# One core, four fused layers: how the attention sums of two query tiles are turned and divided

## The reference, cut to what matters

```
scores = einsum('bhid,bhjd->bhij', q, k) / 4 + alibi        # 16 heads, 2048 x 2048
scores = where(causal, scores, -inf)
attn   = softmax(scores, axis=-1)
out    = einsum('bhij,bhjd->bhid', attn, v)                 # 16 numbers a head
x      = layernorm(x + out.reshape(b, l, 256) @ o_w)
```

## Time and profile before

| | us |
|---|---|
| median of three runs | 1425.99 (1423.18 to 1426.55) |
| the profiled execution | 1421.0 |
| its span in the profile | 1419.2 |
| PE busy | 1369.9 |
| DVE busy | 1064.5 |
| ACT busy | 870.5 |

### The profile page before, as it was taken

One profiled execution on the slowest core, in us unless ns is written; L12 is line 12 of the kernel. 1 busy time (PEld: TensorE's weight loads), 2 busy tenths in 40 slices (PEclk: granted clock), 3 DMA queues, 4 the chain that ended last, 5 costly groups with the idle time before them and its releaser, 6 DMA issues. The chain is left out here.

```text
span 1419.2 us, 44173 instructions
## 1 busy us (share of the span) xinstructions
PE 1369.9 (97%) x18460; PEld 844.3 (59%) x18460; DVE 1064.5 (75%) x2004; ACT 870.5 (61%) x1775; POOL 264.2 (19%) x436
## 2 busy tenths in 40 slices
PE   7999999999999999999999999899997799999998
PEld 4554334444444444444444445687876689999997
DVE  2567888988888888888888881356687676777775
ACT  3445658778787787787787877655465333333332
POOL 4332111102111111121011100000256611111111
PEclk9999999999999999999999999999998799999999
DMA  7695411112212212121300000312705555454441
GB/s 224 206 214 122 84 19 37 46 32 49 47 33 48 46 33 47 34 47 41 83 23 3 3 3 2 117 31 91 258 29 191 209 186 183 179 185 178 164 181 70
DMA packets 77824, 134.08 MB, mean 94 GB/s; under 512 B 12226, under 2 KB 64443, under 8 KB 72252
## 3 DMA queue, kind: packets, MB, share of 16 engines
q1 hardware_dynamic: 59612, 108.84, 25.9%
q10 hardware_dynamic: 14608, 14.00, 3.1%
q0 software_dynamic: 3408, 8.43, 1.7%
HBM read 67.75 MB, written 23.11 MB: 64 GB/s over the span
## 5 line engine op out<-in xcount | busy, mean ns | idle before, releaser
L1611 ACT ACTIVATE big<-pair 128x512 f32<-128x512 f32 (+1 forms) x1120 | 584.9, 600 | 184.3 <-PE pair L1244 175.1
L1799 DVE TENSOR_REDUCE part_max<-pair 128x2 f32<-128x1024 f32 (+2 forms) x576 | 643.2, 1161 | 72.6 <-PE pair L1216 43.6
L1244 PE MATMUL pair<-big 128*32 128x512 bf16 (+3 forms) x5120 | 344.9, 349 | 3.4 <-DMA big<-max_t 2.6
L1216 PE MATMUL pair<-big 128*32 128x512 bf16 (+3 forms) x5120 | 341.0, 349 | 4.5 <-DVE part_max L1799 4.0
L1266 PE MATMUL pair<-big 128*17 128x512 f32 (+3 forms) x2560 | 288.0, 528 | 0.7 <-POOL big L2228 0.3
L1216 PEld LDWEIGHTS pair<-big 128*32 128x32 bf16 x5120 | 124.9, 96 | 185.3 <-DVE part_max L1799 87.7
L1244 PEld LDWEIGHTS pair<-big 128*32 128x32 bf16 x5120 | 123.2, 96 | 157.0 <-ACT big L1611 71.6
L1624 ACT ACTIVATE std<-moments,eps_col 128x1 f32<-128x1 f32 (+1 forms) x110 | 32.5, 295 | 218.4 <-DVE moments L1837 218.3
L1502 PE MATMUL pair<-big,tok 128*128 128x128 f32 x1248 | 147.6, 277 | 4.8 <-DVE big L2112 4.8
L1502 PEld LDWEIGHTS pair<-big,tok 128*128 128x128 f32 x1248 | 146.9, 194 | 7.6 <-DVE big L2112 5.7
L2228 POOL TENSOR_SCALAR_AFFINE_SELECT big<-big 128x512 f32<-128x512 f32 x128 | 80.1, 635 | 331.1 <-ACT big L1611 331.1
(11 more groups left out here) (184 smaller groups left out, 1280.1 us busy)
## 6 DMA issues: line engine op xcount, KB each, us to landing
tok<-big SPq DMA_DIRECT2D x39, 1024.0 KB, 4.7
big<-in_L_ffn_w SPq DMA_DIRECT2D x16, 1024.0 KB, 13.7
big<-split_dram SPq DMA_DIRECT2D x216, 64.0 KB, 2.8
split_dram<-big ACTq DMA_DIRECT2D x32, 384.0 KB, 4.0
big<-split_dram SPq DMA_DIRECT2D x42, 256.0 KB, 4.2
big<-routed_dram SPq DMA_DIRECT2D x39, 129.0 KB, 2.1
tok<-in_L_attn_x SPq DMA_DIRECT2D x8, 512.0 KB, 6.0
big<-in_c_query_rows SPq DMA_DIRECT2D x8, 512.0 KB, 4.8
```

What stands on the lines that cost most here:

```text
L1216: mm = pe.matmul(bank[q:q + STRIPE, o:o + w], m.q_op[slot][:, step.qt, h, step.r * P + q:step.r * P + q + STRIPE], m.k_op[slot][:, h, step ...
L1244: mm = pe.matmul(m.bank[step.bank][k:k + STRIPE, n * w:(n + 1) * w], m.k_op[slot][:, h, step.kb * P + k:step.kb * P + k + STRIPE], m.q_op[ ...
L1611: act.activation(m.p_ring[:, step.place, step.heads[0]:step.heads[-1] + 1, step.at:step.at + w], m.bank[step.bank][:, 0:len(step.heads) * ...
L1799: dve.tensor_reduce(m.part_max[(step.u * QT + step.qt) % 2][:, step.r, step.heads[0]:step.heads[0] + n, step.c], banks[:, :, 0:w], X, ALU. ...
```

## The change

Divide is done once for two query tiles, t even and t + 1, when the sums of the second have been taken. PE then makes eight transposes, four from each `acc_t`, into the two banks of one slot; DVE inverts and multiplies over both banks in one instruction each. The order is planned anew with 1070 ns of PE and 950 ns of DVE for it. POOL waits at the start of the back until the ring has been taken, since `acc_t[0]` is now read by the last Divide.

```
 # FrontPlan.take_sums
-        self.to_divide.append((t, self.sums_at))
+        if t % 2:
+            self.to_divide.append((t - 1, self.sums_at))
 # FrontPlan.divide
-        self.divided_ring[t] = n
-        self.steps.append(Divide(t // QT, t % QT, t, n, room))
-        self.pe += 640
-        self.dve = max(self.dve, self.pe + self.PE_LAG) + 600
+        self.divided_ring[t] = self.divided_ring[t + 1] = n
+        self.steps.append(Divide(t // QT, t % QT, t, t // 2, n, room))
+        self.pe += 1070
+        self.dve = max(self.dve, self.pe + self.PE_LAG) + 950
 # tensor_front
-            a = step.t % 2
-            pe.wait_ge(s.sums_taken, step.t + 1)
+            pe.wait_ge(s.sums_taken, step.t + 2)
             wait_room(pe, s, step.room)
-            for r in range(BPT):
-                mm = pe.transpose(m.bank[MAX_BANKS[step.room.slot][0]][:, r * P:(r + 1) * P], m.acc_t[a][:, r * P:(r + 1) * P],
-                                  m.ident[:, :])
+            for a, b in enumerate(MAX_BANKS[step.room.slot]):
+                for r in range(BPT):
+                    mm = pe.transpose(m.bank[b][:, r * P:(r + 1) * P], m.acc_t[a][:, r * P:(r + 1) * P], m.ident[:, :])
             mm.then_inc(s.ring_filled, 1)
 # vector_front
-            view = m.bank[MAX_BANKS[step.room.slot][0]].rearrange("p (r h n) -> p r h n", r=BPT, h=GH)
+            view = m.max_tile[step.room.slot][:, :].rearrange("p (r h n) -> p r h n", r=2 * BPT, h=GH)
...
-            dve.wait_ge(s.inverted, step.t + 1)
+            dve.wait_ge(s.inverted, step.n + 1)
             dve.tensor_tensor(dst, view[:, :, :, 0:HD], m.recip_l[:, :, :].unsqueeze(3)
-                              .broadcast_to([P, BPT, GH, HD]), ALU.mult).then_inc(s.ring_taken, 1)
+                              .broadcast_to([P, 2 * BPT, GH, HD]), ALU.mult).then_inc(s.ring_taken, 1)
 # pool_back
     pool.wait_ge(s.sums_taken, len(UNITS) * QT)
+    pool.wait_ge(s.ring_taken, plan.front_ring)
     pool.memset(m.ones_b, 1.0).then_inc(s.onesb_set, 1)
```

More of the change, by code:

```diff
@@ L95 @@
 TakeSums = namedtuple("TakeSums", "t weighed divided_before")
-Divide = namedtuple("Divide", "u qt t ring room")
+Divide = namedtuple("Divide", "u qt t n ring room")
 Residuals = namedtuple("Residuals", "ring")
@@ L364, in take_sums @@
         self.sums = None
+        assert t < 2 or t - 2 in self.divided_ring
         self.steps.append(TakeSums(t, weighed, self.divided_ring.get(t - 2, -1) + 1))
@@ L929, in __init__ @@
         self.max_t = [sb(f"max_t{i}", [3 * MAXIMA, P], BF16) for i in range(2)]
-        self.recip_l = sb("recip_l", [P, BPT, GH])
+        self.recip_l = sb("recip_l", [P, 2 * BPT, GH])
         self.stats = sb("stats", [P, NORMS, BPT, 6])
@@ L1040, in __init__ @@
                        for i in range(W1_AHEAD)]
-        self.gate = self.recip_l[:, :, :].rearrange("p a b -> p (a b)")
+        self.gate = self.recip_l[:, 0:BPT, :].rearrange("p a b -> p (a b)")
     def group(self, g):
@@ L1819, in vector_front @@
             b, g = UNITS[step.u]
-            view = m.bank[MAX_BANKS[step.room.slot][0]].rearrange("p (r h n) -> p r h n", r=BPT, h=GH)
+            view = m.max_tile[step.room.slot][:, :].rearrange("p (r h n) -> p r h n", r=2 * BPT, h=GH)
             blk = b * BPB + step.qt * BPT
-            dst = m.tok[:, blk:blk + BPT, g * GH * HD:(g + 1) * GH * HD].rearrange("p r (h n) -> p r h n", h=GH)
+            dst = m.tok[:, blk:blk + 2 * BPT, g * GH * HD:(g + 1) * GH * HD].rearrange("p r (h n) -> p r h n", h=GH)
             dve.wait_ge(s.ring_filled, step.ring + 1)
             dve.reciprocal(m.recip_l[:, :, :], view[:, :, :, HD]).then_inc(s.inverted, 1)
-            dve.wait_ge(s.inverted, step.t + 1)
+            dve.wait_ge(s.inverted, step.n + 1)
             dve.tensor_tensor(dst, view[:, :, :, 0:HD], m.recip_l[:, :, :].unsqueeze(3)
-                              .broadcast_to([P, BPT, GH, HD]), ALU.mult).then_inc(s.ring_taken, 1)
+                              .broadcast_to([P, 2 * BPT, GH, HD]), ALU.mult).then_inc(s.ring_taken, 1)
 def take_moments(dve, m, s, i, rows):
```

## The result

| | before | after |
|---|---|---|
| median, 7 runs each | 1423.18 us | 1415.45 us |
| ratio, with its 95% interval | | 0.9942 [0.9927, 0.9957] |
| profiled execution | 1421.0 | 1415.08 |
| its span | 1419.2 | 1413.3 |

That the gain is twice as large does not come from the base. The size is wrong, and what the size came from is wrong too. In two kernels of the experiments (e10, e12) one execution took 2153 and 2068 us; these two are left out of the ratios.

What follows compares the result with a forecast made beforehand. PE was taken to bound the attention, with ACT beside it from 872 us. PE -3.7, DVE -0.4 and tail net +0.36 summed to -3.7 us: from 1425.99 to 1422.3, range 1416 to 1430.

Steps and rivals of the forecast that it cites:

- the repeating units: Attention's four-tile units of 95.5 us: PE busy 95.2 to 95.45, so only 0.05 to 0.4 us idle to win.
- A pair gives back 0.28 us: PE time saved per merged Divide, taken as 0.26; 14 pairs give 3.64 us, -3.7 with the first pair.
- The plan stays about as true as it was: Planned prices fall 210 ns of PE and 250 of DVE a pair, near the trace's 260 and 430.
- the 11 us of slack a unit: DVE, busy 84.2 of 95.5 us mid-run, hides both its 0.43 us saving and 0.43 us longer wait per pair.
- The multiply at 0.692 us: DVE's multiply over both banks (128x512), priced from a tensor_tensor of that size; bounds 0.425 and 0.85.
- The reciprocal at 0.275: DVE's reciprocal of 32 instead of 16 numbers, at 1.04 ns an element; bounds 0.258 and 0.516 us.
- The tail, +0.72: The last Divide, fully on the path, grows by 0.43 of transposes, 0.02 of reciprocal and 0.27 of multiply.
- The early stretch, -0.4: Between 147 and 190 us PE waits for the ring, so DVE's saving counts there; bounds 0 and -0.7.
- The clock, 2 us either way: The whole back moves some 4 us against the granted clock, so a low stretch may lie elsewhere.
- the order filling holes: Rival, chance 0.20: new order also takes half of PE's 7.6 us idle between 118 and 334 us; 1418.5 us.
- Given back at the ring: Rival, chance 0.18: PE waits for the slot as long as it saved; only the tail left, 1426.4 us.
- The slower rival: Chance 0.12, with other bad orders: maxima come too late, PE waits 1.32 us in 8 more tiles; 1432.9 us.

Runs made afterwards that it cites:

- e10: Changed kernel, its order planned with the merged Divide at 950 ns of PE and 720 of VectorE instead of 1070 and 950; ratio 0.9929 to the kernel before.
- e12: Kernel before, single Divides, its order planned with 750 ns of VectorE instead of 600, PE left at 640; ratio 0.9948 to the kernel before.
- e1: Kernel before's list of steps with even Divides taken out, pairs merged where the odd ones stood, slots handed out anew; ratio 1.0047 to the kernel before.
- e5: Kernel before, single Divides, its order planned with 700 ns of PE and 750 of VectorE instead of 640 and 600; ratio 0.9942 to the kernel before.
- e3: Changed kernel, with VectorE inverting and multiplying each of the two banks by itself; ratio 0.9962 to the kernel before.
- e9: Kernel before, single Divides, its order planned with 800 ns of PE and 900 of VectorE instead of 640 and 600; ratio 1.0027 to the kernel before.
- e14: Kernel before, single Divides, its order planned with 820 ns of VectorE instead of 600, PE left at 640; ratio 1.0016 to the kernel before.

## Why the prediction was wrong, step by step

PE's share in the piece was priced right; the step that failed is the reading that the repeating units had nothing to win.

- "A pair gives back 0.28 us ... I take 0.26": right. The Divides' surcharge fell by 2.6 us over 10 pairs in the old order (e1), by 2.2 in the new.
- "In the repeating units there is next to nothing to win (0.05 to 0.4 us of idle PE a unit)": this step failed. There were 6.7 us of short waits in five units, 1.3 a unit, and 4.7 of them are gone in the changed kernel's order; e12, which changes the order alone, has 1.6 us left and the whole gain. I had written that a busy PE says nothing, looked at a few groups, and then took the busy time for the bound on idleness after all. Added up over the unit, the distances from start to start would have given the 1.3.
- That merging by itself pays, with the order as a risk beside it: failed as well. In the old order the five units are 2.0 us longer with merging (e1), though each Divide costs less. An order alone, with single Divides, gives as much as the change (e5, e12).
- "The plan stays about as true as it was": so it did. VectorE's price fell short of the measured time by 0.24 us for two single Divides, and by 0.14 for a pair. The order changed nearly everywhere all the same.
- "In the middle of the run the 11 us of slack a unit hide both" (VectorE's two times): half right. Splitting VectorE's work again cost 1.7 us in five units (e3), so it is not all hidden.
- The multiply at 0.692 us: right, 0.692. The reciprocal at 0.275: wrong, it is 0.357, since 16 more numbers took 0.099 us, 6.2 ns each, not the multiply's 1.04. I had put the slope of another operation to it; the bounds held it. The pair takes 1.09 on VectorE, saving 0.35 and not 0.43, so 5.6 us over the run. Without the gaps the two instructions add up to 5.0 us less over the run, and VectorE's busy time on the page of the profile, where instructions that overlap count once, fell by 3.6, where I had said 6 to 7.
- The tail, +0.72: 0.80, by that same reciprocal. Net with the last unit I said +0.36; the last unit, which was to win 0.36, lost 0.4.
- The early stretch, -0.4: -0.5 to TakeSums 3. That this has the right size is luck: the granted clock differed there (0.83 against 1.00 between 184 and 194 us), a difference in clock goes with 1.5 us in e5's two profiles, and the new order has its part in it too. No run separates them.
- The clock, 2 us either way: +1.4 net, of -2.7 and +4.1.
- The base: the median before was 1423.18 and not 1425.99 us. My forecast difference from there gives 1419.5, still 4 us too slow.
- The rivals: the one that came nearest was the order filling holes, but I looked for the holes in the early stretch, and capped them there at half of 7.6 us. "Given back at the ring" came in e1's five units, for one half at the ring and for the other at ACT. The slower rival did not come by late maxima; e9 and e14 are slower by more and longer short waits.

The rule of the Trainium skill that I weighed ("Perfetto Trace Analysis", section "Optimizing Scalar/DVE Operations": breaking instructions up may help where Vector isn't saturated and causes bubbles on others) is not borne out here: e3 breaks them up and is 2.4 us longer in the front. It is a weak test, since e3's pieces all wait for the eight transposes and free the slot after the last one, so that nothing is done sooner. Another rule of that page (section "Identifying the Most-Contended Engine") says that the matmuls' busy share is no good measure of how close a kernel is to its roofline. The trace agrees as far as it goes: 95.45 of 95.5 us busy, and 1.5 us a unit were to be had.

## What to carry to other kernels

Where matmuls are pipelined, count idle PE time from start to start, group by group, over a whole period, before saying that nothing is left. Where an order is planned from prices, a change of a piece and a change of the order are two changes: run the old piece under altered prices first, since one number may give the same gain. And a merged piece dropped into an order made for single ones can lose what it saves: in e1 PE only came sooner to a wait for ACT or for a slot. A tool that remakes a list must be looked at as well: in e1 and e2 it gave two banks to the scores later, and the waits there are as long as what was to be measured.

## What the runs showed of the hardware

A reciprocal from PSUM costs 6.2 ns for each further number per partition (16 numbers 0.258 us, 32 numbers 0.357), six times the 1.04 ns of the multiply. And the same back, moved by 7 us, met the granted clock at 0.52 instead of 0.66 over 35 to 39 us of one stretch, and at 1.00 instead of 0.91 in another: with a front that differs by a few us, the back's length is no measure of the change. It isn't from chip to chip either: the changed kernel's back took 522.6 us in one profile and 530.1 in another.
